# Three fp32r products for the full passes of two mixtures of experts, in a ring of 12 slots

## What is computed

```python
out = router_top2_weights(x)           # each of 128 tokens picks 2 of 8 experts
for e in range(8):
    out += w[:, e] * ((silu(x @ Wg[e].T) * (x @ Wu[e].T)) @ Wd[e].T)
```

## Time and profile before

| | us |
|---|---|
| median of 3 runs | 1275.16 |
| the profiled execution, own time | 1277.02 |
| its span | 1275.2 |
| PE busy | 1182.9 (93%) |
| DVE, ACT, POOL busy | 269.2, 206.5, 22.0 |
| DMA, HBM read | 442.38 MB |

### The profile page before, as it was taken

One profiled execution on the slowest core, in us unless ns is written; L12 is line 12 of the kernel. 1 busy time (PEld: TensorE's weight loads), 2 busy tenths in 40 slices (PEclk: granted clock), 3 DMA queues, 4 the chain that ended last, 5 costly groups with the idle time before them and its releaser, 6 DMA issues.

```text
span 1275.2 us, 14376 instructions
## 1 busy us (share of the span) xinstructions
PE 1182.9 (93%) x6011; PEld 621.3 (49%) x6011; DVE 269.2 (21%) x654; ACT 206.5 (16%) x314; POOL 22.0 (2%) x47
## 2 busy tenths in 40 slices
PE   5999999899999999998899798999999899889988
PEld 4677686665433443446655633433344444333434
DVE  7977542422000000004342300000000000000000
ACT  5766312211000000001122100000000000000000
POOL 2000000000000000000000000000000000000000
PEclk9999999999999999999899799999999999999999
DMA  9988646915999999999110399999999999999994
GB/s 376 423 339 339 266 164 243 415 52 213 427 425 426 426 425 425 425 425 424 71 58 1 129 427 425 425 425 425 425 425 425 425 426 425 426 426 425 426 426 194
DMA packets 42287, 443.70 MB, mean 348 GB/s; under 512 B 4736, under 2 KB 4768, under 8 KB 7408
## 3 DMA queue, kind: packets, MB, share of 16 engines
q1 hardware_dynamic: 39312, 427.05, 80.0%
q0 software_dynamic: 2912, 15.74, 3.2%
HBM read 442.38 MB, written 0.39 MB: 347 GB/s over the span
## 4 chain that ended last, share of the span: by engine, by line
PE 87%; DVE 6%; issue 4%; ACT 2%; DMA 1%; POOL 0%; SPq 0%; DVEq 0%
PE PJ L1524 40%; PE TP L1552 12%; PE AC L1552 9%; PE AC L1355 4%; PE AC L1367 3%; PE PJ L1271 2%; PE TP L1534 2%; PE MS L1248 2%; PE PJ L1328 1%; PE TP L1489 1%; DMA ring<-in_weights 1%; PE PJ L1281 1%; PE PJ L1283 1%; PE PJ L1282 1%; DVE extra L824 1%
## 5 line engine op out<-in xcount | busy, mean ns | idle before, releaser
L1046 DVE SCALAR_TENSOR_TENSOR act<-low,CB,PJ 128x512 f32<-128x512 f32 x48 | 35.9, 747 | 755.4 <-PE PJ L1524 755.4
L1524 PE MATMUL PJ<-scratch,picked 128*64 128x512 f32 (+1 forms) x684 | 155.3, 595 | 10.8 <-issue 10.8
L1524 PE MATMUL PJ<-ring,picked 128*32 128x512 f32 (+1 forms) x744 | 151.5, 604 | 10.0 <-issue 10.0
L687 ACT ACTIVATE low<-PJ 128x512 f32<-128x512 f32 x48 | 28.7, 597 | 730.0 <-PE PJ L1524 730.0
L1524 PE MATMUL PJ<-ring,extra 128*128 128x512 f32 x252 | 112.2, 595 | 0.0
L1524 PE MATMUL PJ<-scratch,extra 128*128 128x512 f32 x204 | 90.8, 594 | 0.0
L1524 PEld LDWEIGHTS PJ<-scratch,picked 128*64 128x64 f32 (+1 forms) x684 | 48.9, 127 | 79.4 <-issue 79.1
L1524 PEld LDWEIGHTS PJ<-ring,picked 128*32 128x32 f32 (+1 forms) x744 | 47.2, 122 | 77.6 <-issue 76.7
L1552 PE MATMUL TP<-ring,extra 128*64 128x256 f32 (+3 forms) x528 | 75.3, 488 | 6.0 <-issue 6.0
L1552 PE MATMUL TP<-scratch,extra 128*32 128x512 f32 (+3 forms) x528 | 73.1, 512 | 8.0 <-issue 8.0
L1524 PE MATMUL PJ<-extra,picked 128*32 128x512 f32 (+1 forms) x300 | 69.5, 594 | 4.1 <-issue 4.1
(11 more groups left out here) (327 smaller groups left out, 1218.3 us busy)
## 6 DMA issues: line engine op xcount, KB each, us to landing
ring<-in_weights SPq DMA_DIRECT2D x142, 1536.0 KB, 30.0
scratch<-in_weights SPq DMA_DIRECT2D x99, 1536.0 KB, 37.5
extra<-in_weights SPq DMA_DIRECT2D x30, 1536.0 KB, 37.5
extra<-in_attn POOLq DMA_DIRECT2D x12, 768.0 KB, 9.9
extra<-in_attn POOLq DMA_DIRECT2D x6, 512.0 KB, 9.2
scratch<-in_ffn_vectors POOLq DMA_DIRECT2D x1, 2688.5 KB, 13.1
extra<-in_x SPq DMA_DIRECT2D x1, 384.0 KB, 3.3
out<-extra SPq DMA_DIRECT2D x1, 384.0 KB, 2.3
```

What stands on the lines that cost most here:

```text
L687: A(silu, PJ[:, 0:SEG], ACT.Silu).then_inc(S("silu_ready"), 1)
L1046: v.scalar_tensor_tensor(hexp, silu, weight, PJ[:, SEG:2 * SEG], ALU.mult, ALU.mult) \
L1524: ins = mm(dst[c], x[:, t, c], slab_at(LOAD[q, kind, side])[:, t * SEG:(t + 1) * SEG], start=(t == 0), stop=(t == KT - 1))
```

## The change

Full and shared passes take three fp32r products. ACT (`whole_hi`) rounds half slabs into four half buffers, the memory of slots 10 and 11, which leave the ring. DVE (`whole_lo`) writes the remainder over the slab itself. The tokens and the hidden values are split likewise (`tokens_lo`, `hidden_lo`). Twelve slots remain, and in mixture 1 slot 13 is left out of the first turn. Expert numbers are read when first needed. In mixture 3 the full passes end earlier, so that three pair passes are last; the last two slabs come as eight DMAs of a quarter slab, `down` waits for them quarter by quarter, and the last adding, copying and storing go in two halves. Pairs keep their fp32 products. `picks` moves from `low[1]` to H1.

```diff
+CLOSING = {1: 1, 3: 4}
...
-    places = {round(i * (total - 1) / (fulls - 1)): i for i in range(fulls)}
+    places = {round(i * (total - CLOSING[l]) / (fulls - 1)): i for i in range(fulls)}
-    1: [0, 1, 8, 9, 10, 11, 2, 3, 4, 5, 6, 7, 12, 13],
-    3: [0, 1, 2, 3, 4, 5, 8, 9, 10, 11, 6, 7, 12, 13],
+    1: [0, 1, 8, 9, 2, 13, 3, 4, 5, 6, 7, 12],
+    3: [0, 1, 2, 3, 4, 5, 8, 9, 6, 7, 12, 13],
+LATER = {1: [13], 3: []}
+    opening = [s for s in TURN[l] if s not in LATER[l]]
+    return opening[k] if k < len(opening) else TURN[l][(k - len(opening)) % len(TURN[l])]
...
@@ sync: mixture @@
+                            sp.wait_ge(S("shares_made"), 1 if l == 1 else 2)
-                        expert = [sp.value_load(sid[0:1, r:r + 1], min_val=0, max_val=E8 - 1) for r in range(E8)]
+                        expert[rank] = sp.value_load(sid[0:1, rank:rank + 1], min_val=0, max_val=E8 - 1)
+                    if n >= N_SLABS - 2:
+                        closing.append((n, expert[rank] * (3 * m["per"]) + (m["slab"] + 3 * j + kind)))
+                        continue
+                for t in range(4):
+                    for n, index in closing:
+                        part = slice(t * D, (t + 1) * D)
+                        sp.dma_start(slab_at(n)[:, part], weights[index, :, part]) \
+                            .then_inc(S(f"closing_landed_{t}"), 16)
...
@@ scalar: mixture @@
+                def whole_hi(q, kind, both=(0, 1)):
...
+                    landed(act, n)
+                    for half in both:
+                        step = 2 * HI[n] + half
+                        if step >= 4:
+                            name, value = HI_USED[step - 4]
+                            act.wait_ge(S(name), value)
+                        A(hi_half(n, half), half_slab(n, half), ACT.Copy).then_inc(S("whole_hi"), 1)
+                if l == 1:
+                    whole_hi(0, "g")
                 transposed(k)
+                A(XTh[:].rearrange("p k n -> p (k n)"), TP[:, 0:D], ACT.Copy).then_inc(S("XTh_ready"), 1)
+                if l == 1:
+                    whole_hi(0, "u", (0,))
...
                 for q in range(m["first"], LAST_PASS[l] + 1):
+                    whole_hi(q - 1, "d")
                     silu_of(q)
...
+                    whole_hi(q + 1, "g")
+                    whole_hi(q + 1, "u")
+                whole_hi(LAST_PASS[l], "d")
                 hidden_turned(LAST_PASS[l])
...
@@ vector: mixture @@
+                if l == 1:
+                    whole_lo(0, "g")
...
+                    tokens_lo()
                     dve.wait_ge(S("router_exp"), nth + 1)
...
+                if l == 1:
+                    whole_lo(0, "u", (0,))
+                else:
+                    tokens_lo()
                 dve.wait_ge(S("counted"), nth + 1)
...
                 v.tensor_copy(sid[:], r8[:, 8, :]).then_inc(S("order_ready"), 1)
+                if l == 1:
+                    whole_lo(0, "u", (1,))
...
                 for q in range(m["first"], LAST_PASS[l] + 1):
+                    whole_lo(q - 1, "d")
+                    hidden_lo(q - 1)
+                    whole_lo(q + 1, "g")
                     hidden(q)
+                    whole_lo(q + 1, "u")
...
+                whole_lo(LAST_PASS[l], "d")
+                hidden_lo(LAST_PASS[l])
...
-            take_x(8, None)
+            for a, b in halves():
+                v.tensor_copy(Y_copy[:, a:b], Y[:, a:b]).then_inc(S("pair_copied"), 1)
+            for i, (a, b) in enumerate(halves()):
+                dve.wait_ge(S("pair_added"), 6 + i)
+                v.tensor_copy(X[:, a:b], AC[:, a:b]).then_inc(S("x_ready"), 1)
...
@@ tensor: mixture, up @@
+                    if what != "pair":
+                        pe.wait_ge(S("tokens_lo"), nth + 1)
...
+                            if t % 3 == 0:
+                                pe.wait_ge(S("whole_lo"), 2 * HI[n] + half + 1)
+                            mm(dst, XT_lo[:, t, :], hi[:, w], start=(t == 0), stop=False)
+                            mm(dst, XTh[:, t, :], lo, start=False, stop=False)
+                            ins = mm(dst, XTh[:, t, :], hi[:, w], start=False, stop=(t == KT - 1))
+                            if t == 2:
+                                ins.then_inc(S("hi_half_used"), 1)
```

## The result

The changed kernel took 1283.08 us (median of 5 runs, 1281.33 to 1284.61) against 1275.16: the ratio is 1.0059, with a 95% interval of 1.0047 to 1.0070. It is slower by 7.9 us, more than the 0.3% that a measurement of this kernel can tell, and lies 2 us over the range. The profiled execution took 1283.21 us, with a span of 1281.4 and a mean granted clock of 0.968 (before: 1275.2, 0.987).

A forecast was written before the change was run, and what follows sets the result against it. DMA bounds mixture 3; in mixture 1 PE's chain and the loads are tied by the ring. Mixture 1 +5.0, clock +1.5, mixture 3's start -3.4, end -4.7: -1.6 us, 1273.6 against the median 1275.16; range 1262 to 1281.

The forecast's parts named there:

- What bounds the kernel: Mixture 3 is bound by full DMA at 425 GB/s; in mixture 1 PE's products and the loads end 14 us apart.
- The products: Full passes: three fp32r products cut a pass from 15.5 to 12.4 us; nine in mixture 1 save 27 us of PE.
- The opening: Start of mixture 1: PE waits 4 us twice behind gathers; d2 ends at 348.7 instead of 347.2, losing 1.5 us.
- The ring: Mixture 1, 12 slots: slab 20 waits for d2, 9 us without transfer; last slab lands at 579.3, 6.9 us later.
- The clock: Opening of mixture 1: two new 4 us waits, each costing 1.65 us of half clock at half chance: +1.5 us.
- The end of mixture 1: Last down of mixture 1 follows DVE's copy and remainders; the mixture ends at 591.3 instead of 586.3, +5.0 us.
- Rival B: Mixture 1, g1 to g2: clock at 0.50 for 16 to 20 us, 8 to 9 us lost; 1281 us, chance 0.2.
- Rival A: Opening of mixture 1: the splits hide, d2 ends near 339, mixture 1 near 581.8; 1262.6 us, chance 0.2.
- Rival C: Mixture 3: one read takes as long as eight, or quarters flow 3 us slower; 1277 us, chance 0.1.
- The start of mixture 3 and the end: One read instead of eight before mixture 3's first DMA, -3.4 us; quarter slabs and halves after the last transfer, -4.7 us.

The follow-up runs named there:

- the run with the full clock: Changed kernel plus small useless matmuls in TensorE's waits of mixture 1, counts fitted to the waits (6, 17, 17, 13, 9): 1276.70 us, ratio 0.9989.
- ACT's order turned: Changed kernel with ScalarE's rounding of pass 1's and 2's gate slabs put ahead of the copies of gathers 0 and 2: 1273.13 us, ratio 0.9975.

## Why the prediction was wrong

**What bounds the kernel**: right. Mixture 3 went at 425 GB/s with 12 slots, and its splits changed nothing there (the run with plain products in mixture 3).

**The products**: right in size (18 at a pitch of 0.23, a down of 4.16 to 4.2 us), and of little worth. With all repairs of order and plain products mixture 1 ends at 587.0, with splits at 586.6, with splits and useless matmuls at 583.9: the 27 us less of PE work brought 0.4 to 3.1 us, for the loads are the limit right behind.

**The opening**: the order of events was right, and both waits of 4 us were where it had them; d2 came 3.8 us late (352.5 for 348.7), and the run with the full clock ends it at 349.4.

**The ring**: right in mechanism. Slab 20 waited behind d2, and the hole ended there. That the ring alone made mixture 1 5.2 us late is not a proof of the forecast's +5.0, which was worked out with the splits in the chain; for the ring alone I had expected 1 us, since 14 us between loads and products would hide the lag, and that was wrong.

**The clock, the step that failed.** The forecast says "Each at 3.3 us of half clock costs 1.65 us; half the chance for each", **+1.5 us**. Measured it is about 7.5: that much earlier does mixture 1 end with the full clock. Of the 9.7 us that mixture 1 took beyond the forecast's 6.5, this term is 6.0. The price of one wait was right: by the pitches g0, g1, g2, g17 and the last down lost 1.6, 1.6, 1.4, 2.5 and 1.8 us (g1 took 5.97 us for 4.40 with the full clock; the 2.0 that I had put down for it before the useless matmuls was too much). Wrong was the count, two waits in place of five. The wait before g0 (1.58 us) stood in my schedule (286.0 for 284.2), the one before g17 (3.40 us, its slab landing late and being rounded) only in "From about 485 us on PE waits for slabs", and neither got a clock; that before the last down I had priced as time alone. Of the opening's 4.6 us of half clock 3.1 arrive at d2 and 3.5 at the last slab's landing, since slab 20's slot passes them on to the stream.

The half chance was too low for long waits and fair for short ones. In mixture 1 of the kernel after the clock fell behind all five waits of over 3 us (two of them, 3.64 us before 491.85 and 3.69 before 548.76, stand in the run with the full clock as well, so the 7.5 us hold nothing of them). Behind shorter ones it fell twice (1.58 and 2.31 us) and stayed at 1.00 three times (1.49, 1.52 and 1.70); with ACT's order turned it fell behind the 1.58 again and stayed at 1.00 behind 1.75, 2.31 and 2.34 us. The Trainium skill (TensorE: Matmul & The Clock Gate, HAM oscillation) describes half clock behind each wait for a transfer between short groups of matmuls. The trace agrees in so far as it shows 0.52 and 0.57 behind two waits at the end of mixture 1; these were waits for remainders made by DVE.

**The end of mixture 1, the other part.** 591.3 forecast, 595.0 with the full clock: 3.7 us remain. The forecast had the last slab land at 579.3; ACT takes it up, on landing, at 586.94, and at 583.42 in the run with the full clock. From there to the end it took 11.6 us for the forecast's 12.0, so that all of the 3.7 lies in the stream. The forecast had one hole of 9 us; there were several smaller ones besides (between 306 and 342 us the DMA engines of the kernel after moved 262 to 406 GB/s in each 6 us). I put them down to releases before d2 that were late too: with ACT's order turned the figures are 369 to 435 up to 336 us.

**Rival B** is nearly what happened: +9 us of half clock, 1281 us, passed on by slab 20. It had 0.2 and a place that was too narrow: not 16 us at 0.50 in one stretch, but five of about 4 us, two of them at the end of the mixture. Its bound, d2 5.4 us later than forecast, wasn't met (3.8), so that I would have called it wrong by its own mark. **Rival A** needs no wait behind the gathers; with ACT's order turned, d2 comes at 343.8. **Rival C**: no; one read takes 0.98 us with what is around it, and the quarters moved 396 GB/s.

**The start of mixture 3 and the end**: -3.8 and -5.0 for -3.4 and -4.7. The Trainium skill (DMA: Bandwidth & Descriptors, Measured) has 78% of peak for a transfer of 1 MB and 32% for one of 64 KB, issued by POOL; the prediction took the 78% for its strips of 384 KB. The eight of them, queued by SP, moved 396 GB/s between 1259 and 1266 where the slabs move 425, which is 93%. Here the measurement decides.

## What to carry to other kernels

When a cheaper product brings preparation by other engines with it, write down the order of their queues in the stages with no slack, and there look for a step that waits for PE and stands ahead of one that PE waits for: moving two lines of ACT's program was worth 13.3 us here, 4.2 of them clock, and more than anything that the new products gave. Price every new wait of PE twice, as time and as the half clock that can follow it, the small ones too; where a wait can't be removed, matmuls of no use that fit inside it (measure one first) gave 7.5 us. If a ring gets shorter, look which slab waits for the slot that comes free last: three slots exchanged paid for two slots lost.

## What the runs showed of the hardware

- In mixture 1 of the kernel after, PE having been busy before each wait, the clock went to 1.2 GHz behind waits of 1.58, 4.2, 4.2, 3.6, 3.7, 3.4 and 2.3 us, and stayed there for some 2 to 6 us of products; it stayed at 1.00 behind waits of 1.49, 1.52 and 1.70. With ACT's order turned it stayed at 1.00 behind the same wait of 2.31 us. So the length of the wait alone doesn't decide. With small fp32 matmuls in the waits it stayed at 1.00. Stretches behind a wait of 3.64 and one of 1.70 us (kernel after), and behind that of 2.31 (ACT's order):

```profile
491.80:496.50 4.70, 4.65 (x19) 4.04 (x20) 0.65 (x1) 0.00 (x0) 0.00 (x0) 0.67 1.00 419
522.00:526.00 4.00, 3.94 (x16) 2.96 (x17) 0.00 (x0) 0.00 (x0) 0.00 (x0) 1.00 1.00 421
```

```profile
584.70:589.20 4.50, 4.42 (x26) 3.93 (x27) 0.03 (x1) 0.00 (x0) 0.00 (x0) 1.00 1.01 426
```

- Such a matmul, 128x128 in fp32, shows as two records and takes 0.22 us.
- The stages between the mixtures, with the same instructions, took 127.2 to 131.0 us in different profiles, at a granted clock of 0.99 to 0.96. That is the size of half the change's effect, so that only stretches could be compared.
- In mixture 3 PE of the kernel after waits for the hidden remainder before almost every full down, and its granted clock there is 0.93 to 0.97 in stretches of 100 us, for 0.97 to 1.00 in the kernel before; the stream hides both (waits from 740 to 1255 us):

```profile
PE AC L1688 <- DVE extra_lo L1150: 31.8, 12, 3.7
PE PJ L1662 <- DMA ring<-in_weights: 7.0, 5, 2.2
```
